# Six of sixteen attention products on GpSimd, and every engine's list in a new order

## The reference

```
x = x + attn_a(layernorm(x))   # 8 heads: projections, rotation by a cumulated angle, a linear recurrence over time, rms norm, projection
x = x + ffn(layernorm(x))      # one 128x128 product with a ternary weight, and a bias
x = x + attn_b(layernorm(x))   # 16 heads of 8 channels: softmax attention, for each time step over the 8 batch rows
x = x + ffn(layernorm(x))
```

```
scores = einsum('sbhd,tbhd->bhst', q * scale, k)
attn   = softmax(scores, axis=-1)
out    = einsum('bhst,tbhd->sbhd', attn, v).reshape(S, B, E)
return out @ out_proj_w.T + out_proj_b
```

## Time and profile before

| | us |
|---|---|
| median of 3 runs (lowest to highest) | 645.05 (643.44 to 648.27) |
| profiled execution, its device time | 646.3 |
| span of the profiled execution | 644.5 |
| PE, DVE, ACT, POOL busy in the span | 542.1, 493.8, 482.2, 390.6 |
| mean granted TensorE clock | 0.947 |

### The profile page before, as it was taken

How to read it: one execution, slowest core, us unless ns; L and a number is a source line. 1 busy time by engine, 2 the same in 40 slices (tenths; PEclk the granted TensorE clock), 3 DMA queues, 4 the chain that set the end, 5 groups by cost and what they waited for, 6 DMA issues and landing times.

```text
span 644.5 us, 13428 instructions
## 1 busy us (share of the span) xinstructions
PE 542.1 (84%) x3952; PEld 448.1 (70%) x3952; DVE 493.8 (77%) x1096; ACT 482.2 (75%) x1472; POOL 390.6 (61%) x530
## 2 busy tenths in 40 slices
PE   5969999999998779879998788898997777878177
PEld 4847788888776667668777577786776665766166
DVE  6666756787679999947759999877579899541985
ACT  3899999999978578878987568699988588623101
POOL 7358889988756366657656456578656265520431
PEclk9999999999999899989999889899999798978688
DMA  8641212312111103122111002222111111010001
GB/s 202 191 120 50 91 54 75 106 56 72 55 57 55 28 31 95 51 73 73 55 55 55 22 36 71 72 72 74 60 50 55 56 55 52 1 33 1 0 0 34
DMA packets 52325, 39.43 MB, mean 61 GB/s; under 512 B 7318, under 2 KB 48027, under 8 KB 52251
## 3 DMA queue, kind: packets, MB, share of 16 engines
q1 hardware_dynamic: 44858, 34.86, 18.3%
q10 hardware_dynamic: 7392, 3.67, 2.0%
HBM read 33.44 MB, written 4.46 MB: 59 GB/s over the span
## 4 chain that ended last, share of the span: by engine, by line
PE 33%; DVE 29%; ACT 15%; issue 12%; POOL 5%; DMA 3%; SPq 2%; DVEq 1%; ACTq 0%; POOLq 0%
PE ps L1474 6%; ACT turned L845 4%; ACT turned L830 4%; PE ps L1697 3%; DVE area L1257 3%; DVE area L1253 3%; DVE area L1245 3%; PE ps L1706 3%; PE ps L1643 3%; PE ps L1803 3%; DVE lmat L1149 2%; DVE area L1239 2%; DVE state L1188 2%; DMA xt<-xT_rows 2%; PE ps L1624 2%
## 5 line engine op out<-in xcount | busy, mean ns | idle before, releaser
L845 ACT ACTIVATE turned<-ps,sct 128x128 f32<-128x128 f32 x376 | 107.5, 422 | 17.3 <-PE ps L1518 17.3
L830 ACT ACTIVATE turned<-ps,sct 128x128 f32<-128x128 f32 x376 | 108.7, 426 | 15.5 <-PE ps L1518 15.3
L595 POOL TENSOR_TENSOR bn<-turned 128x256 f32<-128x256 f32 x64 | 51.2, 800 | 91.0 <-ACT turned L830 56.1
L1149 DVE TENSOR_TENSOR_SCAN lmat<-arow,band 128x512 f32<-128x512 f32 x64 | 93.2, 1457 | 8.3 <-POOL band L616 7.4
L736 ACT ACTIVATE area<-ps 128x256 f32<-128x256 f32 (+1 forms) x68 | 35.0, 557 | 65.6 <-PE ps L1803 26.7
L1611 PE MATMUL ps<-cT,bT 128*128 128x128 f32 x512 | 69.9, 279 | 10.6 <-issue 6.2
L1611 PEld LDWEIGHTS ps<-cT,bT 128*128 128x128 f32 x512 | 63.7, 192 | 18.9 <-issue 17.1
L595 POOL TENSOR_TENSOR cn<-turned 128x256 f32<-128x256 f32 x64 | 50.9, 795 | 38.9 <-ACT turned L845 38.3
L1157 DVE TENSOR_TENSOR mmat<-ps,lmat 128x512 f32<-128x512 f32 x64 | 43.8, 684 | 36.9 <-PE ps L1611 34.3
L1516 PE MATMUL ps<-w_sel_hi,xt_hi 128*128 128x512 f32 x128 | 59.6, 466 | 3.7 <-DVE xt_lo L1141 3.7
L616 POOL TENSOR_TENSOR band<-bandm,sct 128x512 f32<-128x512 f32 x47 | 53.5, 1139 | 14.8 <-DMA sct<-packed 11.5
(11 more groups left out here) (233 smaller groups left out, 1405.3 us busy)
## 6 DMA issues: line engine op xcount, KB each, us to landing
arow<-alpha_rows SPq DMA_DIRECT2D x32, 512.0 KB, 3.8
drow<-decay_rows SPq DMA_DIRECT2D x64, 128.0 KB, 3.0
area<-in_L_attn_a_x_dram SPq DMA_DIRECT2D x4, 512.0 KB, 5.9
xT_rows<-turned SPq DMA_DIRECT2D x4, 512.0 KB, 5.2
xt<-xT_rows SPq DMA_DIRECT2D x32, 64.0 KB, 2.4
area<-in_L_attn_a_x_dram ACTq DMA_DIRECT2D x8, 256.0 KB, 3.4
out_dram<-area ACTq DMA_DIRECT2D x6, 256.0 KB, 2.3
area<-L_attn_a_sel_proj_w_dram SPq DMA_DIRECT2D x2, 512.0 KB, 6.5
```

The costliest lines, as they stand in the source:

```text
L595: pool.tensor_tensor(out[:, 0], zc[:, 0], zs[:, 1], ALU.subtract)
L830: last = act.activation(dst[h][:, N * q:N * q + N], bank(BK_B)[:, N * q:N * q + N], ACT.Copy, scale=scalars(c, k)[:, at + HH * h + q:at + ...
L845: last = act.activation(dst[h][:, N * q:N * q + N], bank(BK_C)[:, N * q:N * q + N], ACT.Copy, scale=scalars(c, k)[:, at + HH * h + q:at + ...
L1149: dve.tensor_tensor_scan(lmat[h], arow[i2][:, HH * P * h:HH * P * (h + 1)], band[h], 0.0, ALU.mult, ALU.add).then_inc(l_dve, 1)
```

## The change

Three things are changed.

**Six products move.** `ON_GPSIMD = [3, 11, 6, 7, 14, 15]`: two of the eight query products and four of the eight value products of every chunk but the last go to a new function `f_product` on POOL. They write a ring of three buffers, `g_ring`, in the SBUF tile `small`, which the prologue alone used. Since POOL gets its operands from SBUF, ACT copies the query rows 3 of each half from the accumulator (`qcopy`, `q_row`), and DVE writes the weights of two tiles, already multiplied with the reciprocal sums, to `w_pair` at the end of `norms`. `onorm` covers two tiles in place of four. The sixteen reductions stay on DVE; six of them wait for `g_prod`. The tail of chunk 3 is as it was.

```diff
+ON_GPSIMD = [3, 11, 6, 7, 14, 15]
+ON_VECTOR = [m for m in range(2 * NB) if m not in ON_GPSIMD]
...
+            def f_product(c, m):
+
+                g, at = m // NB, ON_GPSIMD.index(m)
+                if at >= 3:
+                    pool.wait_ge(f_red, 2 * NB * c + ON_GPSIMD[at - 3] + 1)
+                if m % NB < 4:
+                    for part in range(2):
+                        pool.wait_ge(f_q[part], 2 * c + 2)
+                    pool.wait_ge(f_row[g], c + 1)
+                    pool.tensor_tensor(by_row(g_ring[at % 3]), query_of(q_row[g]), ks, ALU.mult).then_inc(g_prod, 1)
+                else:
+                    pool.wait_ge(f_weights[g], c + 1)
+                    weights = w_pair[g][:, P * (m % 4 - 2):P * (m % 4 - 1)].rearrange("p (h r) -> p h r", r=NB)
+                    pool.tensor_tensor(g_ring[at % 3].rearrange("p (h d r) -> p h d r", r=NB, d=AD),
+                                       weights.unsqueeze(2).broadcast_to([P, AH, AD, NB]),
+                                       vals.rearrange("p (h d) r -> p h d r", d=AD), ALU.mult).then_inc(g_prod, 1)
...
+            def f_query_row(c, g):
+
+                act.wait_ge(f_pe[g], use_done(("Q", g), c))
+                evac(q_row[g], q_bank(g)[:, 3 * D:4 * D]).then_inc(f_row[g], 1)
...
+                dve.wait_ge(f_v[g], v_step("rec", c))
+                dve.tensor_tensor(w_pair[g].rearrange("p (s r) -> p s r", r=NB), q_bank(g)[:, 2 * P:4 * P].rearrange("p (s r) -> p s r", r=NB),
+                                  asum[:, 4 * g + 2:4 * g + 4].rearrange("p s h -> p (s h)").unsqueeze(2).broadcast_to([P, 2 * AH, NB]),
+                                  ALU.mult).then_inc(f_weights[g], 1)
```

**The table `PLACE` is new** throughout, of which two entries show the manner:

```diff
-         "red1": 22.05, "Q1": 22.059, "prod2": 22.1, "prod3": 22.35, "red2": 22.55, "red3": 22.575,
+         "prod0": 21.8, "prod1": 21.833, "red0": 22.103, "red1": 22.138, "prod2": 22.276, "prod3": 22.333,
```

More of the change, by code:

```diff
@@ L64 @@
 XSTEPS = ["x1", "ffn0", "attn", "ffn1"]
-PLACE = {"rr:0": 10.583, "load:0": 12.708, "x1:0": 14.425, "var0:0": 14.875, "rs0:0": 15.333, "xn0:0": 15.647,
[17 rows of a table removed]
+PLACE = {"rr:0": 11.467, "load:0": 13.741, "x1:0": 14.931, "var0:0": 15.533, "xn0:0": 15.815, "T0": 15.9,
[17 rows of a table added]
 ENDING = {f"{n}{m}" for m in range(2 * NB) for n in ("prod", "red")}
-ENDING |= {f"{n}:{g}" for g in range(2) for n in ("softmax", "exp", "norms", "onorm", "var2", "rs2", "xn2", "store")}
+ENDING |= {f"{n}:{g}" for g in range(2) for n in ("qcopy", "softmax", "exp", "norms", "onorm", "var2", "rs2", "xn2", "store")}
 ENDING |= {f"{n}{t}" for t in range(4, 8) for n in ("T", "tout")}
@@ L391, in hybrid_block @@
             small[:, k, :] for k in range(24))
+        g_area = small[:].rearrange("p a b -> p (a b)")
+        g_ring = [g_area[:, 1024 * k:1024 * k + 1024] for k in range(3)]
+        q_row = [g_area[:, 3072 + D * g:3072 + D * (g + 1)] for g in range(2)]
+        w_pair = [g_area[:, 3328 + 2 * P * g:3328 + 2 * P * (g + 1)] for g in range(2)]
         def tiles(a):
@@ L655, in ln_root @@
                 pool.tensor_tensor(sh_f[:, half(g)], sh_f[:, half(g)], rs, ALU.mult).then_inc(f_g[g], 1)
+            def f_product(c, m):
[13 more added lines that the diff above has]
+                                       vals.rearrange("p (h d) r -> p h d r", d=AD), ALU.mult).then_inc(g_prod, 1)
             pieces = []
+            for m in ON_GPSIMD:
+                place(pieces, f"prod{m}", lambda c, m=m: f_product(c, m))
             for g in range(2):
@@ L925, in _ @@
             for g in range(2):
+                place(pieces, f"qcopy:{g}", lambda c, g=g: f_query_row(c, g))
                 place(pieces, f"exp:{g}", lambda c, g=g: f_softmax_exp(c, g))
@@ L934, in step @@
                     if ok(k + 1, 1):
+                        c_turn(c, k + 1, 0)
+                    at_span(pieces, c, k, 0.125, 0.312, first)
+                    if ok(k + 1, 1):
+                        c_turn(c, k + 1, 1)
+                    if ok(k):
+                        cT_out(c, k)
+                    if ok(k - 2):
+                        y_square(c, (k - 2) // 2)
+                    at_span(pieces, c, k, 0.312, 0.688, first)
+                    if ok(k + 2, 1):
+                        u_out(c, k + 2)
@@ L948, in step @@
                         c_turn(c, k + 1, 1)
[L949 to L965 removed]
+                    at_span(pieces, c, k, 0.519, 0.593, first)
@@ L966, in step @@
                     if ok(k + 3, 1):
                         x_high(c, (k + 3) // 2)
[L968 to L974 removed]
+                    at_span(pieces, c, k, 0.593, 0.704, first)
@@ L977, in _ @@
+                    if ok(k + 2, 1):
+                        b_turn(c, k + 2, 0)
+                    at_span(pieces, c, k, 0.704, 0.852, first)
+                    if ok(k + 2, 1):
+                        b_turn(c, k + 2, 1)
+                    if ok(k + 1):
+                        bT_out(c, k + 1)
+                    at_span(pieces, c, k, 0.852, 1, first)
             act.wait_ge(xT_first, 16)
@@ L1289, in _ @@
                 place(pieces, f"add{what[0]}{what[1]}", lambda c, what=what: f_add(c, what))
+            for m in ON_VECTOR:
+                place(pieces, f"prod{m}", lambda c, m=m: f_product(c, m))
             for m in range(2 * NB):
-                place(pieces, f"prod{m}", lambda c, m=m: f_product(c, m))
                 place(pieces, f"red{m}", lambda c, m=m: f_reduce(c, m))
@@ L1765, in step @@
+                    if ok(k + 2, 1):
+                        project_c(c, k + 2)
+                    at_span(pieces, c, k, 0.722, 0.833, first)
+                    if ok(k + 1):
+                        turn_b(c, k + 1)
+                    at_span(pieces, c, k, 0.833, 0.944, first)
+                    if ok(k) and has_state(c, k):
+                        states(c, k)
+                else:
                     if ok(k - 1):
                         outputs(c, k - 1, not first or k - 1 >= FIRST_INTER)
-                    at_span(pieces, c, k, 0.381, 0.476, first)
@@ L1768, in step @@
-                    if ok(k - 1) and has_state(c, k - 1):
-                        states(c, k - 1)
-                    at_span(pieces, c, k, 0.476, 0.571, first)
+                    at_span(pieces, c, k, 0, 0.25, first)
                     if ok(k):
                         turn_c(c, k)
-                    at_span(pieces, c, k, 0.571, 0.714, first)
+                    at_span(pieces, c, k, 0.25, 0.4, first)
+                    if ok(k + 2, 1):
+                        project_b(c, k + 2)
@@ L1782, in operands_ready @@
+                    if ok(k + 2, 1):
+                        project_c(c, k + 2)
+                    if ok(k + 1):
+                        turn_b(c, k + 1)
+                    at_span(pieces, c, k, 0.8, 1, first)
             def operands_ready():
```

185 lines of the change are left out of this document (75 added, 110 removed), and 32 rows, old and new, of the table PLACE.

## The result

The changed kernel took **614.37 us** as a median of 4 runs (612.06 to 616.17), against 645.5 of the kernel before beside it. The ratio is 0.951, 95% interval 0.946 to 0.956: 31 us faster, where 10 were forecast. The profiled execution took 614.7 us, and its span is 612.9 where it was 644.5.

The account below looks back on a forecast made before the run. No engine bounds the whole, but DVE bounds units 6 to 13 of chunk 1. 646.3 - 12.2 + 3 (hold) + 1 (branch) = 638.1, or 636.9 on the median's scale, less 2 for the clock: 635 us, range 617 to 649.

Parts of the forecast that it names:

- a difference of two sums: Chunks 1 to 3: sums before less sums after, 3.8, 3.8 and 4.6 us, taken off the profiled 646.3 us: -12.2.
- the prediction's sums: Per pair of units, the larger of DVE's and PE's sums, over eight pairs: 136.3 us before, 132.5 after.
- the 3 us over in chunk 1: Chunk 1 before measured 139.18 us against its sum of 136.3; the 3 us over were placed at the entry.
- A new order cannot win in chunk 0: Chunk 0 left as it is, since PE and ACT are full under the old order; 94 to 95 us expected.
- The hold: Units 6 to 13: DVE and POOL hold each other up, scans meeting POOL's products; 1 us a chunk, +3 in all.
- The branch: Behind the loop's branch, a scan and a `y_of` stand ahead of the `mmat` PE needs: +1 us, once.
- the 2 us of the clock: PE less idle in units 6 to 13, so part of its lower clock may come back: 2 us taken off.
- POOL's cover for `red6` and the rest: `red6`, `red7`, `red14`, `red15` stand behind POOL's products; no added wait, with 1.7 us of cover.
- Rival (a): More gain: engines even out over more than a pair, a chunk tends to PE's 124 us; 620 us, chance 0.18.
- (b): No gain: reordered lists lose in PE-bound units what DVE gains; 643 to 648 us, chance 0.24 with (d).
- (d): No gain: reductions wait for POOL's products in `small`, bounded by 1.7 us; time of (b), chance 0.24 with (b).
- (c): Slower: each of 18 POOL products holds a scan or other two-input instruction for 2.1 us; 672 us, chance 0.13.

Follow-up runs that it names:

- e5_move_behind: Kernel before, old lists, with six products moved to POOL, the value products placed behind `wu` and `bn`: 653.10 us, ratio 1.013.
- e3_warm: Kernel before with four more transposes on PE ahead of the wait for `mmat` in units 6 to 13 of chunks 1 to 3: 649.38 us, ratio 1.006.
- e2_move: Kernel before, old lists, with only the six products moved to POOL, at the places first tried: 656.39 us, ratio 1.018.
- e8_seven: Changed kernel with chunks 1 and 2 written out and product 10 on POOL as a seventh, three buffers kept: 639.53 us, ratio 0.991 to before.
- e10_old_dve: Changed kernel with only DVE's recurrence steps in the order of before: 705.35 us, ratio 1.094 to before.
- e14_old_act: Changed kernel with only ACT's recurrence steps in the order of before: 692.41 us, ratio 1.072 to before.
- e6: Kernel before with `T4` later in PE's list, behind its urgent work, `tout4` and `O0` moved with it: 643.19 us, ratio 0.995.
- e7: Kernel before with the changes of e5_move_behind and e6 together: 652.06 us, ratio 1.010.
- e13: e5_move_behind with DVE's products 4, 5, 12 and 13 put behind `mmat`, `red15` and `onorm` behind the scan: 665.44 us, ratio 1.029 to before.
- e16: e13 with `T4` and `T5` later in PE's list, and `tout`, `O` and add of both moved with them: 654.89 us, ratio 1.010 to before.

## Why the prediction was wrong

**Right.** Units 6 to 13 of chunk 1 were forecast at 66 to 68 us with DVE over 95% busy: 67.0 and 97%. All eight scans there take 1.21 us, no reduction of `small` waits, POOL's products take 2.37 us (for value products 1.97 or 2.36 was open), and POOL is busy for 52.7 us, below 55.

**The step that failed is the one that put a difference of two sums on the measured time of before**, which leaves that kernel's own excess over its sum where it was. By the prediction's sums, units 0 to 13 of a chunk are 121.0 us before (136.3 less the last pair), 111.5 in chunk 3. Measured: 123.4, 125.8 and 119.6. After: 117.2 and 107.5 by the sums, 117.5, 117.3 and 107.3 measured. (For chunk 3 the prediction has totals alone, 127.7 and 123.1. 111.5 and 107.5 are from the same working, whose pairs it does not show; with 15.3 for the last pair, as in the other chunks, they would be 112.4 and 107.8.) The sums were right for the changed kernel to within 0.3 us, in chunk 1 partly by luck: 0.4 too high in units 0 to 5, 0.7 too low in 6 to 13. The excess of 2.4, 4.8 and some 8 us was gone, and 0.8 in the last pair of chunk 2. That is 16 us. Neither half removes it alone: under the new lists without the move, e1_order, units 0 to 13 of chunks 1 and 2 take 124.8 and 126.6 us where the sums of its expectation give 123.6 (138.9 less 15.3), so 1.2 and 3.0 of excess stay. The prediction saw the 3 us over in chunk 1, put them down to the entry and looked no further; in chunk 3 it held its sum against nothing. Put in place of the measured stretches, the sums of after give 646.3 - (123.4 - 117.2) - (142.3 - 132.5) - (119.6 - 107.5) = 618 us. (A slip in the sums changes none of this: 122.7 less 19 leaves 13.0 a pair for the recurrence, not 13.1, in both kernels alike.)

**"A new order cannot win in chunk 0"** failed too, on a size: 73.1 became 71.4 us. PE's 12.04 busy of 12.2 was not all work: after, two pairs in its midst take 11.84 each with PE busy for 11.54, over as many matmuls in the whole stretch (536 and 537). ACT is busy for all 71.4 us, as against 71.6 of 73.1, and is full alone. In the same way "units 0 to 5 not shorter" fell, 52.6 to 50.5.

**The added waits.** The hold was to cost 3 us through POOL's products. No product delays a scan, since the new lists keep them apart. `onorm` stands beside `bn` instead in chunks 1 and 2 and takes 0.96 us three times and 1.67 once, 0.48 and 0.51 in chunk 3, where 0.42 is its shortest in e5_move_behind: 3.0 us over the six. That is the size forecast, by another instruction, so by luck. On balance the hold added nothing: over chunks 1 to 3 the DVE instructions with both operands in SBUF took 12 us more than their shortest, and 13 before (scans 7.7 and now 2.6 of it, `xt_lo` 0.6 and now 2.1, `onorm` 0.3 and now 2.6 over its own shortest). The branch was to cost 1 us more; its pair exceeds that of chunk 2 by 5.3 us after and by 6.9 before, so 1.6 less. For the 2 us of the clock no run shows a term: e3_warm had 14 us less at half clock and won nothing. POOL's cover for `red6` and the rest held: no reduction of `small` waits in the changed kernel.

**Rival (a)** came nearest in time (620), by another mechanism than its own: chunks didn't tend to PE's 124 us but to the pair sums, 132.9 in chunk 2. Its "8 to 12 below now" was against the pair sums too; chunk 2 had stood 18 above. **(b)** and **(d)** name what e2_move, e8_seven, e10_old_dve and e14_old_act show: with the same instructions, places decide over -31 to +60 us. **(c)** is real as a mechanism (below) and small as a term.

**What is shown and what stays open.** Shown: order alone 0, move alone +8 to +11 with the places tried, both -31. In the changed kernel DVE is 96 to 98% busy in units 6 to 13, and three products and then three more taken off each count. That the new lists let the freed time through because they fit each other is argued from e10_old_dve and e14_old_act, not shown by itself. Not settled is why the old lists can't use the room: taking out one stall after another (e5, e6, e7, e13, e16) moved it on each time, and the places for POOL's products in them were mine, not searched for.

## What to carry to other kernels

Where engines run from fixed lists, hold the sum of the larger engine per stretch against the measured time of every stretch, and ask of the excess whether the change redoes the lists. If it does, the new sum is the lower end of the forecast and the difference of the sums the upper one: this change came within 0.3 us of its sums, order alone within 1 to 3. Moving work to another engine without redoing the lists may give nothing or cost time: here the freed engine only waited longer. Count buffers for moved work by what frees them: one too few cost 35 us here, and each moved product had brought 1.6 (29.3 over 18).

## What the runs showed of the hardware

A scan that begins during a POOL product ends when the product has ended and the scan's own time has passed. In e5_move_behind, POOL and DVE:

```profile
201.62 2.82 POOL L675 TENSOR_TENSOR small<-small,area 128x1024 f32<-128x1024 f32 x1
204.41 1.96 POOL L625 TENSOR_TENSOR band<-bandm,sct 128x512 f32<-128x512 f32 x1
...
202.74 2.78 DVE L1183 TENSOR_TENSOR_SCAN lmat<-arow,band 128x512 f32<-128x512 f32 x1
```

The scan takes 2.78 us instead of 1.21 and ends 1.08 after the product; `band` behind it takes 1.96 instead of 1.05. All nine such meetings in e2_move, e5_move_behind and e7_both read 2.78 or 2.79. In e14_old_act, where the scan begins later in the product, three read 1.98 to 2.01, and in the changed kernel one that begins 0.13 us ahead of the product's end reads 1.21; in all of them the scan ends 1.08 us after the product. This is what the Trainium skill ("SBUF — State Buffer", section on the two separate sides) says of the shared port pair, that the instruction of the two engines which begins first has it to its end and the other is blocked. Products and reductions of DVE beside POOL's products stayed at 1.20 to 1.23: a product there reads one operand from an accumulator and a reduction has one input.

The loop's one branch back costs 5 to 7 us here, more than the 3.7 us for which PE waits behind it: the pair across it fell from 21.0 to 15.7 us with the chunks written out, and in the kernel before it takes 6.9 us more than the same pair of chunk 2.
